# Where the chain of small steps hangs between attention and experts, and VectorE's blocks in it cut into single steps

## The reference

```
def _L0(x, mask, conditioning, Wq, Wk, Wv, Wo, rms_scale, Wc, bc):   # 16 heads of 16
    scores = jnp.einsum('bhsd,bhtd->bhst', q, k) * scale
    scores = jnp.where(mask[None, None, :, :], -jnp.inf, scores)
    out = softmax(scores) @ v, heads joined, @ Wo.T
    xn = out / rms(out) * rms_scale
    xn = xn * (1.0 + sc[:, None, :]) + shift[:, None, :]
def _L1(x, ...):                       # 8 experts, the best 2 for each token
    gate = rmsnorm(x) @ wg_W + wg_b + (genre_embed @ gg_W + gg_b)
    topk_w, topk_i = jax.lax.top_k(softmax(gate), 2)
    h1 = relu(x @ W1[e] + b1[e]); h2 = relu(h1 @ W2[e] + b2[e]); out = h2 @ W3[e] + b3[e]
    sum of the two outputs by topk_w
def _L2(x, ...): x @ basis.T, scaled per batch, @ orthogonalised 64x64 matrix, @ output basis
def _L3(x, ...): quaternion rotation of x by normalised q_left and q_right
x = x + _L0(...); x = x + _L1(...); x = x + _L2(...); x = x + _L3(...)
```

## Time and profile before

| | us |
|---|---|
| median of 3 runs | 1307.14 (1304.28 to 1310.64) |
| profiled execution | 1312.69 |
| its span | 1310.9 |
| TensorE busy | 1188.8 (91%) |
| VectorE busy | 977.5 (75%) |
| ScalarE busy | 620.0 (47%) |
| GpSimd busy | 544.8 (42%) |
| mean granted clock | 0.965 |

### The profile page before, as it was taken

One profiled execution on the slowest core, in us unless ns is written; L12 is line 12 of the kernel. 1 busy time (PEld: TensorE's weight loads), 2 busy tenths in 40 slices (PEclk: granted clock), 3 DMA queues, 4 the chain that ended last, 5 costly groups with the idle time before them and its releaser, 6 DMA issues.

```text
span 1310.9 us, 23750 instructions
## 1 busy us (share of the span) xinstructions
PE 1188.8 (91%) x7523; PEld 778.1 (59%) x7580; DVE 977.5 (75%) x2711; ACT 620.0 (47%) x1199; POOL 544.8 (42%) x865
## 2 busy tenths in 40 slices
PE   4599999799999999999957899999999899999968
PEld 2233343334433343433414798999999898899958
DVE  2687887778797888878744778777777888866647
ACT  2166665556665556555533333433333333344435
POOL 4424236646665656656463645232221221212220
PEclk9799999999999999999988999999999999999989
DMA  6573636526547374553612649963564664722536
GB/s 180 158 220 120 202 121 198 173 86 205 178 152 204 116 210 142 179 171 119 240 57 94 218 137 305 314 171 59 170 188 131 182 204 120 247 48 42 166 81 193
DMA packets 99332, 213.12 MB, mean 163 GB/s; under 512 B 10822, under 2 KB 69702, under 8 KB 90375
## 3 DMA queue, kind: packets, MB, share of 16 engines
q1 hardware_dynamic: 84902, 192.92, 45.3%
q0 software_dynamic: 14304, 18.69, 8.0%
HBM read 240.32 MB, written 75.84 MB: 241 GB/s over the span
## 4 chain that ended last, share of the span: by engine, by line
PE 69%; DVE 12%; issue 7%; POOL 6%; ACT 3%; DMA 2%; SPq 1%; another core or an unknown queue 0%; POOLq 0%; DVEq 0%; ACTq 0%
PE bank L925 28%; PE bank L1021 8%; PE bank L990 8%; PE bank L1002 6%; PE bank L1006 5%; PE bank L963 4%; PE bank L1039 2%; DVE full L1562 2%; DVE ab L730 2%; POOL routed L1749 2%; PE bank L939 2%; DVE junk L1422 1%; PE bank L971 1%; DVE osb L1461 1%; DMA stacks<-split_parts 1%
## 5 line engine op out<-in xcount | busy, mean ns | idle before, releaser
L1422 DVE CUSTOM_DVE_ANT_0 junk<-bank,mneg 128x512 bf16<-128x512 f32 x512 | 333.8, 686 | 84.8 <-PE bank L990 84.1
L1173 ACT ACTIVATE pt<-bank 128x512 f32<-128x512 f32 x512 | 302.5, 595 | 191.7 <-PE bank L1006 133.3
L1759 POOL DMA_INDIRECT x<-yout,rows x78 | 122.5, 1570 | 350.1 <-ACT yout L1235 296.9
L925 PE MATMUL bank<-hid,w 128*128 128x256 f32 x1872 | 240.2, 285 | 9.3 <-DVE hid L1565 9.3
L1230 ACT ACTIVATE hid<-bank,biases 128x256 fp32r<-128x256 f32 x312 | 147.1, 474 | 195.8 <-PE bank L925 195.4
L925 PEld LDWEIGHTS bank<-hid,w 128*128 128x128 f32 x1872 | 227.2, 190 | 18.1 <-DVE hid L1565 11.4
L1562 DVE TENSOR_SCALAR full<-bank,biases 128x256 f32<-128x256 f32 x312 | 149.3, 479 | 55.6 <-ACT hid L1230 55.2
L1006 PE MATMUL bank<-mneg,identb 128*128 128x512 bf16 x391 | 150.6, 385 | 0.0
L1565 DVE TENSOR_TENSOR hid<-full,hid 128x256 fp32r<-128x256 f32 x312 | 135.1, 433 | 10.8
L925 PE MATMUL bank<-rowsT,w 128*128 128x256 f32 x936 | 127.9, 285 | 6.8 <-DVE hid L1565 5.1
L1021 PE MATMUL bank<-pt,vaug 128*17 128x512 f32 x1024 | 128.3, 620 | 4.6 <-DVE turned L1438 3.5
(11 more groups left out here) (177 smaller groups left out, 1508.0 us busy)
## 6 DMA issues: line engine op xcount, KB each, us to landing
w<-split_weights SPq DMA_DIRECT2D x80, 1024.0 KB
w<-split_weights SPq DMA_DIRECT2D x40, 2048.0 KB
split_weights<-w_parts SPq DMA_DIRECT2D x64, 512.0 KB, 4.4
w_parts<-in_W SPq DMA_DIRECT2D x64, 256.0 KB, 4.5
split_parts<-parts SPq DMA_DIRECT2D x32, 384.0 KB, 2.6
stacks<-split_parts SPq DMA_DIRECT2D x48, 256.0 KB, 5.6
rows<-routed SPq DMA_DIRECT2D x39, 258.0 KB, 3.5
qst<-split_parts SPq DMA_DIRECT2D x24, 256.0 KB, 4.9
```

The costliest lines, as they stand in the source:

```text
L925: product = T.matmul(ps, w[p], x[q], start=(k == 0 and n == 0), stop=(k == len(weights) - 1 and n == 2))
L1173: A.activation(pt[n % len(pt)][:, :], bank[3 + n % 2][:, :], ACT.Exp, scale=float(D) ** -0.5).then_inc(exped.sem, 1)
L1422: V.tensor_tensor_reduce(junk[n % 2][:, :], bank[n % 3][:, :], mneg[:, 0, st, :], 1.0, FLOOR, ALU.add, ALU.max, rowmax[gi % 2][:, hh, st:s ...
L1759: G.indirect_dma_start(x2_dram, bass.IndirectOffsetOnAxis(ap=rows[j % NS][:, tt, E + 1:E + 2].bitcast(U32), axis=0), yout[j % 2][:, tt], N ...
```

## The change

1. Chain hooks in attention stand in all slots for i < 32, in every other slot (n odd) for i = 32 and 33, and nowhere for i = 34.
2. The four output projections of batch 7 no longer stand in front of the first tile. They are among the experts, one per hook, after the rest of chain 6 and ahead of chain 7.
3. In the chain, adding the shift to the input rows is a step of its own (`shift_rows`), each of the four squares has a slot of its own, each of the four scalings too, and each of the second squares. The chain is eight hooks longer.
4. The remainder of a projection (`rest`) is taken out of `project` and stands in the first slot of the next k, `part` in the third.
5. `normalise` is cut in three: turning at (k, n) = (1, 1), `divide` at (1, 3), `turn_back` at (2, 0); it stood after the last slot of k = 1.

```diff
--- before.py
+++ after.py
@@ -115,19 +115,25 @@
 
 def chain(b, out):
 
+    out.append(("shift_rows", b))
+    for st in range(ST):
+        yield
+        out.append(("square_o", b, st))
     out.append(("residual", b))
     for _ in range(6):
         yield
+    for st in range(ST):
+        out.append(("scale", b, st))
+        yield
     out.append(("normalised", b))
-    for _ in range(8):
+    for _ in range(6):
         yield
     for k in range(KT):
         yield
         out.append(("turn_x1", b, k))
     for st in range(ST):
         out.append(("square_x1", b, st))
-        if st % 2:
-            yield
+        yield
     out.append(("root_x1", b))
     for _ in range(4):
         yield
@@ -226,7 +232,7 @@
     def finish_steps(b):
         return [("modulation", b)] + [("project_o", b, st) for st in range(ST)] + [("chain", b)]
 
-    chains, todo, parted = [], [], []
+    chains, todo, rests, parted = [], [], [], []
 
     def work_off():
         step = todo.pop(0)
@@ -235,10 +241,10 @@
         else:
             out.append(step)
             if step[0] == "project":
-                parted.append(("part",) + step[1:])
+                rests.append(("rest",) + step[1:])
 
     for step in project_steps(0):
-        out.extend((step, ("part",) + step[1:]))
+        out.extend((step, ("rest",) + step[1:], ("part",) + step[1:]))
     out.extend(value_steps(0))
     out.append(("constants",))
     for i in range(GROUPS + 3):
@@ -267,12 +273,21 @@
                 if n == 2 and k % 2 == 0 and 0 <= g < GROUPS:
                     out.append(("weigh", g, kt))
                     out.append(("weigh", g, kt + 1))
-                if n == 1 and parted:
+                if n == 0 and rests:
+                    step = rests.pop(0)
+                    out.append(step)
+                    parted.append(("part",) + step[1:])
+                if n == 2 and parted:
                     out.append(parted.pop(0))
-                if chains and next(chains[0], chains) is chains:
+                if 0 <= i - 3 < GROUPS:
+                    if (k, n) == (1, 1):
+                        out.append(("normalise", i - 3))
+                    elif (k, n) == (1, 3):
+                        out.append(("divide", i - 3))
+                    elif (k, n) == (2, 0) and i % 2 == 0:
+                        out.append(("turn_back", i - 3))
+                if (i < GROUPS or i < GROUPS + 2 and n % 2) and chains and next(chains[0], chains) is chains:
                     chains.pop(0)
-            if k == 1 and 0 <= i - 3 < GROUPS:
-                out.append(("normalise", i - 3))
             if k == 1 and 0 <= i - 1 < GROUPS:
                 out.append(("maxima_rows", i - 1))
             n, step = divmod((i - 1) * ST + k, 2)
@@ -310,8 +325,6 @@
     for j in range(3, NS):
         fetch_rows(j)
     out.append(("quaternions",))
-    for st in range(ST):
-        out.append(("project_o", B - 1, st))
     out.append(("turn", 0))
     for m in range(HT):
         out.append(("layer1", 0, m))
@@ -405,6 +418,9 @@
     def later(chains):
         for rest in chains:
             yield from rest
+        for st in range(ST):
+            writer.append(("project_o", B - 1, st))
+            yield
         yield from chain(B - 1, writer)
 
     chains = attention_order(writer)
@@ -584,13 +600,13 @@
     ab_high = signal("ab_high", [(b,) for b in range(B)])
 
 
-    rests = signal("rests", projects)
+    rests = signal("rests", of("rest"))
     gains = signal("gains", of("modulation"))
     max_found = signal("max_found", rows_at)
     cleared = signal("cleared", of("clear"))
     normal = Count(sem("normal"), [(at, 3 + at[0] % 2) for at in of("normalise")])
-    squares = Count(sem("squares"), [(s, 4 if s[0] == "residual" else 1) for s in order if s[0] in ("residual", "square_x1")])
-    scaled = Count(sem("scaled"), [(at, ST) for at in of("normalised")])
+    squares = Signal(sem("squares"), [s for s in order if s[0] in ("square_o", "square_x1")])
+    scaled = signal("scaled", of("scale"))
     PICKS = {"gate_max": 1, "gate_norm": 2, "pick": 2, "picked": 2, "index": 1}
     gate_dve = Count(sem("gate_dve"), [(s, PICKS[s[0]]) for s in order if s[0] in PICKS])
     masks_made = sem("masks_made")
...
@@ -848,7 +864,7 @@
                     sp.wait_ge(*chunk_stored(c))
                 for layer, (a, z) in enumerate(W_COLS):
                     start(w[0][:, a // CW:z // CW].bitcast(U32), split_weights[0, :, a // CW:z // CW]).then_inc(dma_layer[layer][0], 16)
-            elif name == "residual":
+            elif name == "shift_rows":
                 if at[0] == 0:
                     load_xin(1)
             elif name == "normalised":
@@ -1375,10 +1391,10 @@
 
         for step in order:
             name, *at = step
-            if name == "project":
+            if name == "rest":
                 b, qk, half = at
                 n = project_place[b, qk, half]
-                ps, _ = misc_bank(step)
+                ps, _ = misc_bank(("project", *at))
                 dve.wait_ge(*projected.at((b, qk, half)))
                 dve.wait_ge(*high.at((b, qk, half)))
                 if n >= 2:
...
@@ -1429,37 +1445,42 @@
                 V.scalar_tensor_tensor(pr[:, :], mneg[:, 1, kt, :], -MASKED, pr[:, :], ALU.add, ALU.min).then_inc(cleared.sem, 1)
             elif name == "normalise":
                 gi, = at
-                b, u = gi // NG, gi % 2
-                tn, rd = turned[u], rden[u]
+                u = gi % 2
+                tn = turned[u]
                 n = normal.value[gi,] - 3 - u
                 dve.wait_ge(*weighed_all(gi))
                 if n:
                     dve.wait_ge(normal.sem, n)
                 V.transpose(tn[:, :, :].rearrange("p a c -> p (a c)"), bank[5][:, :]).then_inc(normal.sem, 1)
+            elif name == "divide":
+                gi, = at
+                u = gi % 2
+                tn, rd = turned[u], rden[u]
+                n = normal.value[gi,] - 3 - u
                 dve.wait_ge(normal.sem, n + 1)
                 V.reciprocal(rd[:, :], tn[:, :, D]).then_inc(normal.sem, 1)
                 dve.wait_ge(normal.sem, n + 2)
                 V.tensor_tensor(turned[0][:, :, u * D:(u + 1) * D], tn[:, :, 0:D],
                                 rd[:, :].unsqueeze(2).to_broadcast([P, 16, D]), ALU.mult).then_inc(normal.sem, 1)
-                if u:
-                    dve.wait_ge(normal.sem, n + 3)
-                    if b >= 2:
-                        dve.wait_ge(*o_projected.at((b - 2, ST - 1)))
-                    V.transpose(oT[b % 2][:, gi % NG // 2, :], turned[0][:, :, :].rearrange("p a c -> p (a c)")).then_inc(normal.sem, 1)
-            elif name == "residual":
-                b, = at
-                dve.wait_ge(*o_ready.at((b, ST - 1)))
+            elif name == "turn_back":
+                gi, = at
+                b = gi // NG
+                dve.wait_ge(*normal.at((gi,), 1))
+                if b >= 2:
+                    dve.wait_ge(*o_projected.at((b - 2, ST - 1)))
+                V.transpose(oT[b % 2][:, gi % NG // 2, :], turned[0][:, :, :].rearrange("p a c -> p (a c)")).then_inc(normal.sem, 1)
+            elif name == "square_o":
+                b, st = at
+                dve.wait_ge(*o_ready.at((b, st)))
                 if b:
                     dve.wait_ge(*rooted.at(("residual", b - 1)))
-                for st in range(ST):
-                    square(ssq[:, 0, st:st + 1], osb[:, st, :], squares.value[step] - ST + st)
-            elif name == "normalised":
-                b, = at
+                square(ssq[:, 0, st:st + 1], osb[:, st, :], squares.value[step] - 1)
+            elif name == "scale":
+                b, st = at
                 dve.wait_ge(*rooted.at(("residual", b)))
                 dve.wait_ge(*gains.at((b,)))
-                for st in range(ST):
-                    V.scalar_tensor_tensor(osb[:, st, :], osb[:, st, :], ssq[:, 3, st:st + 1], gain[b % 2][:, :],
-                                           ALU.mult, ALU.mult).then_inc(scaled.sem, 1)
+                V.scalar_tensor_tensor(osb[:, st, :], osb[:, st, :], ssq[:, 3, st:st + 1], gain[b % 2][:, :],
+                                       ALU.mult, ALU.mult).then_inc(scaled.sem, 1)
             elif name == "square_x1":
                 b, st = at
                 dve.wait_ge(*rooted.at(("normalised", b)))
@@ -1657,17 +1678,19 @@
                 pool.wait_ge(*w_high.at((c,)))
                 G.tensor_tensor(w_parts[n][:, 1], w_parts[n][:, 1].bitcast(F32), w_parts[n][:, 0].bitcast(F32),
                                 ALU.subtract).then_inc(w_low.sem, 1)
-            elif name == "residual":
+            elif name == "shift_rows":
                 b, = at
                 pool.wait_ge(dma_xin[b % 2], 16 * (b // 2 + 1))
                 pool.wait_ge(*shifts.at((b,)))
                 rooted_step(G.tensor_tensor, xin[b % 2][:, :, :], xin[b % 2][:, :, :],
```

(6 more changed lines are left out.)

## The result

The changed kernel takes 1287.99 us (median of 4 runs, 1286.03 to 1289.37), the kernel before, run beside it, 1306.12 us. The ratio is 0.984, with a 95% interval from 0.982 to 0.987 (it is taken from the single runs; the quotient of the two medians is 0.986). The forecast was 1288 us. The profiled execution took 1289.37 us (span 1287.6, mean clock 0.971); that of before took 1312.69 us, more than any of its timed runs, so of the 23 us between the two spans some 5 us are variation.

A forecast was written before the change was run, and what follows sets the result against it. PE was taken to bound the kernel almost everywhere, except between 650 and 714 us. Hooks -11 us (-21 + 7.2 + 3) and single steps -8 us gave -19, 1288 us against the median, range 1270 to 1303.

The forecast's parts named there:

- The seam: Between attention and experts: batch 5's scatters set the start, first expert rows 20 us earlier, third turning of rows 21 us earlier.
- What is paid later: Among the experts, where PE has no idle time: moved work costs 7.2 us and holes from two chains 3 us.
- the extra 3: Among the experts: chains 6 and 7 both run there and make holes for PE, +3 us, between 0 and 8.
- Single steps: In attention: VectorE's blocks cut into single steps no longer use up PE's three row banks, -8 us, between 0 and -24.
- the split: GpSimd's split of row maxima: batch 0's 4.7 us hole goes, +4 us for later scatters in four batches.
- the cover: Time between the end of GpSimd's split and PE's use of it: 7.3 us before, forecast to shrink to 0.3 us.
- part 2: The single steps in attention: -4.7 - 2.8 - 4.5 + 4 = -8 us, between 0 and -24.
- Single steps gain nothing: Rival for attention: GpSimd's instructions hold each single step as they held the block; only the seam's -11 stays, 1296 us, chance 0.13.
- The slower rival: In attention: scatters come too late for the split of the maxima, a hole in five batches, +13, 1320 us, chance 0.09.
- Everything goes: Rival: the dense part loses its whole excess and the seam its best case, -35 us, 1272 us, chance 0.17.
- the signs of being right: Included no PE wait for batch 6's transpose, rows some 20 us earlier, PE idle under 17 us from 200 to 650 us.
- those of being wrong: PE waiting for the split once per batch, rows late past 700 us, several holes over 2 us, SyncE waiting for the late table.

The follow-up runs named there:

- hooks_only: The kernel before with only the thinner chain hooks and batch 7's projection among the experts: 1299.14 us, ratio 0.994 to the kernel before.
- blocks_again: On the third chip, the changed kernel with squares, scalings and second squares each in one block again, all hooks kept: 1309.41 us, ratio 0.993 to before.
- last_apart: The changed kernel with batch 7's output projection ahead of the first expert tile again, into its own buffer: 1307.42 us on the third chip, ratio 0.993.
- hooks_old: The changed kernel with the old condition on chain hooks in attention, batch 7's projection still among the experts: 1291.88 us, ratio 0.987 to before.
- rest_old: The changed kernel with the projections' remainders formed at once again, at their old place: 1292.43 us, ratio 0.988 to the kernel before.
- norm_whole: The changed kernel with the normalising in one block again behind the last slot of k = 1: 1285.87 us, ratio 0.985 to the kernel before.
- blocks: On the second chip, the changed kernel with squares, scalings and second squares each in one block again, all hooks kept: 1313.08 us, ratio 0.994.

## Why the prediction was right

**The total.** That 1288 was met so closely is luck. The hooks alone gave 8 us by the ratios or 10 by the medians (`hooks_only`) where 11 were forecast, and the rest of the change 12 or 8 where 8 were forecast. Both parts are of the forecast size, and what each is off by cancels.

**The seam.** Right in mechanism, and in size nearly. Batch 5's scatters set the start: SyncE waited 3.5 us more for them after the last normalising. The first one starts 25.5 us after the last row product, where the working had it at 671.3 + 2 - 650.3 = 23. The third turning comes 63.7 us after the last row product, the very figure, but of two terms that were each off by some 1.2 us. From the last row product to SyncE's asking for the first rows it was 57.2 us (707.48 us) and is 38.1, so 19.1 us less instead of 20.3; from there to the third turning it was 27.8 us and is 25.6, so 2.2 less instead of 1. That the loads set this second stretch isn't shown for the changed kernel: no wait for a load stands ahead of its third turning, though one of 0.40 us does in `blocks_again`. The projection could leave the stretch or stay (`last_apart`, 63.3 us) because it fits into PE's wait for the first rows.

**What is paid later.** 7.2 + 3 = 10.2 us were forecast, 587.7 - 575.6 = 12.1 us came. The 7.2 us of work are there (the four projections take 1.02 us each, at 760 to 769 us), so the extra 3 were sized too low: about 5. Behind the third turning PE waits 22.9 us for VectorE's additions to `hid` instead of 14.3, and 2.5 us for eliminations instead of 7.0. Several holes over 2 us were named as a sign that this term is off, and there are two (3.24 and 2.62 us). The first, on GpSimd, VectorE and PE:

```profile
793.65 2.39 POOL L746 TENSOR_TENSOR xw<-xin,osb 128x1024 f32<-128x1024 f32 x1 [4.43 <-DVE osb L1482]
795.99 2.53 POOL L1700 TENSOR_TENSOR xw<-xin,osb 128x1024 f32<-128x1024 f32 x1
```
```profile
792.74 0.43 DVE L1586 TENSOR_TENSOR hid<-full,hid 128x256 fp32r<-128x256 f32 x1
...
793.99 2.33 DVE L1586 TENSOR_TENSOR hid<-full,hid 128x256 fp32r<-128x256 f32 x1
796.24 0.47 DVE L1583 TENSOR_SCALAR full<-bank,biases 128x256 f32<-128x256 f32 x1
796.75 2.05 DVE L1586 TENSOR_TENSOR hid<-full,hid 128x256 fp32r<-128x256 f32 x1
```
```profile
798.95 4.58 PE L941 MATMUL bank<-hid,w 128*128 128x256 f32 x24 [3.24 <-DVE hid L1586]
```

It is the chain's two long additions on GpSimd. VectorE's additions beside them take 2.33 and 2.05 us instead of 0.43, and each ends 0.28 us after GpSimd's, while the instruction between them, which reads PSUM, takes its usual 0.47. This bears out the rule of the Trainium skill ("SBUF — State Buffer", Who interferes with whom).

Together the seam and what lies behind it give -21.3 + 12.1 = -9.2 us (forecast -11); `hooks_only` alone -7.6, `hooks_old` against the changed kernel -5.2.

**Single steps.** The sign was right and the size near, 8 to 12 us instead of 8; its terms were not right. In the two traces the last row product comes 14.1 us sooner. `hooks_only`, whose order there is that of before, has it 5.4 us later than the changed kernel but 8.7 us sooner than the traced execution of before. So what one execution varies by (or one chip, which isn't known for these two) is as large as the term. By the timed ratios it is 0.994 - 0.984, some 12 us, and these intervals are apart. By the medians it is 18.1 - 9.7 = 8.4 us. Its parts by the lists of waits of before and after: row maxima -8.0 (forecast 2.8 + 4.5 = 7.3); the split -3.2 (forecast -4.7 + 4; the cover did go, but each of the four waits stayed at 0.4 us or less); waits for copies +8.4 and the start of attention -5.3, both without a term in the working, and the start goes with the remainders' new place (`rest_old`); smaller waits -2.0. That makes -10.1 us. Undone singly, the remainders cost 4 us, the squares and scalings 3, neither clear of noise, and the normalising nothing. So the group's gain is shown, and which step brings how much of it isn't.

The waits for copies stand in no term of part 2; of them the prediction says only, against a rival, "the transfers and ScalarE's copies that PE also waits for stay". That PE's earlier arrival turned 2.2 us into 10.6 isn't shown: `norm_whole`, where PE arrives earlier still (633.4 us), waits 4.2.

**The rivals.** "Single steps gain nothing" rested on GpSimd's instructions. Two kinds of single steps did meet more of them, from 200 to 650 us (the group's busy time and mean in ns), before and after:

```profile
L1442 DVE TENSOR_TENSOR turned<-turned,rden 128x256 f32<-128x256 f32 x22 | 9.3, 425 | 0.8
L1276 DVE CUSTOM_DVE_ANT_0 squared<-osb 128x256 bf16<-128x256 f32 x20 | 7.3, 418 | 0.0
```
```profile
L1463 DVE TENSOR_TENSOR turned<-turned,rden 128x256 f32<-128x256 f32 x23 | 23.1, 1003 | 0.8
L1292 DVE CUSTOM_DVE_ANT_0 squared<-osb 128x256 bf16<-128x256 f32 x20 | 16.4, 819 | 0.0
```

Twice as long and more, 23 us of VectorE's time. But the scalings, from which the rival argued, did not: their mean fell from 685 to 613 ns. Nor is it the cutting alone. The normalising product still takes 751 ns where it stands in one step again (`norm_whole`), so GpSimd's work has moved beside it; the squares, in a block again (`blocks`), are back at 417. PE's waits for row maxima fell all the same. That a single step of 1 to 2 us delays one row, and three banks cover it, would explain this; it was argued and not measured apart. The rival's premise held in part and its conclusion fell. The slower rival's premise held too (the cover is gone), and its holes didn't come; four slots more don't speak on it, since they put the chunk in front. "Everything goes" fell: 10.6 us of waits for copies and 3.7 for row maxima are left. Of the signs of being right, one was missed narrowly: PE was idle for 18.1 us in attention, not under 17. Of those of being wrong, two came in small: a wait for the split in four batches, and the two holes above.

## What to carry to other kernels

Count from a fixed event (here the last row product) and not from the start of the trace: the stretch from there was met to the tenth, while the same event itself moved by 9 us between two executions of the same order. Where a total is met exactly, look whether its terms were. Give a step that waits for another engine (here the remainders) a later slot. Cutting a block on the engine that feeds PE's banks into single steps lowers the waits for them, even where some of the steps become slower; here it gave 3 us, not clear of noise, and nothing for the normalising. Look which transfer is due next: what is no longer waited for in one place can be waited for in another. Work moved out of an engine's idle stretch is paid in full where it has none, and moving it back doesn't return it if what follows it moves forward too.

## What the runs showed of the hardware

The gain depended on the measurement: 18 us of 1306 in the first, 12 of 1318 on the third chip, for the same two kernels, with gaps in the third's trace that no semaphore explains. GpSimd's scatters start 1.27 us after one another in 39 of 49 cases of the changed kernel, and 1.34 to 1.86 us in the others, mostly from the first of eight to the second; from the first start to the end of the eighth it is 10.0 us in batch 5. SyncE's load that waits for them follows 2.6 us after the last.

A VectorE instruction that takes both inputs from SBUF waited for a GpSimd instruction with two such inputs if that one had begun. In the changed kernel 11 of 23 normalising products (200 to 650 us) start while one runs. They take 1.05 to 2.20 us and each ends 0.28 us after it; the other 12 take 0.42 or 0.43. VectorE, then GpSimd:

```profile
291.12 2.20 DVE L1463 TENSOR_TENSOR turned<-turned,rden 128x256 f32<-128x256 f32 x1
```
```profile
290.68 2.36 POOL L746 TENSOR_TENSOR xw<-xin,osb 128x1024 f32<-128x1024 f32 x1
```

The other way round it is GpSimd that waits. In the kernel before, five of the 22 begin 0.01 or 0.02 us ahead of GpSimd's subtraction. They take 0.42 or 0.43 us, and the subtraction takes 1.54 or 1.55 us instead of 1.27:

```profile
327.84 0.42 DVE L1442 TENSOR_TENSOR turned<-turned,rden 128x256 f32<-128x256 f32 x1
```
```profile
327.86 1.54 POOL L1658 TENSOR_TENSOR w_parts<-w_parts 128x512 fp32r<-128x512 f32 x1
```
